# Windowed attention, cross attention and experts in one kernel: the order of row 0's and each pair's stack transfers

## The reference, cut to what matters

```python
x = x + pos_emb[:S][None]
w = x.reshape(B, nW, WIN, H, hd)                     # windows of 128 tokens, 16 heads of 16
attn = softmax(einsum('bnqhd,bnkhd->bnhqk', w, w) * scale)
local = einsum('bnhqk,bnkhd->bnqhd', attn, w)
comp = conv_general_dilated(x.transpose(0, 2, 1), conv_w, window_strides=(4,), ...) + conv_b
gt = concatenate([comp[:, :G], broadcast(global_memory)], axis=1)   # 64 compressed + 64 memory tokens
ga = softmax(einsum('bshd,bghd->bhsg', xm, gt) * scale)
glob = einsum('bhsg,bghd->bshd', ga, gt)
mix = sigmoid(concatenate([local, glob], -1) @ gate_w + gate_b)
return (mix * local + (1.0 - mix) * glob) @ out_w + out_b
```

## Time and profile before

| what | us |
|---|---|
| three timed runs | 1131.73, 1133.57, 1128.36 |
| median | 1131.73 |
| the profiled execution's own time | 1133.69 |
| its span, first to last instruction | 1131.9 |
| PE busy in the span | 1067.5 (94%) |
| self attention, to the first work of the cross attention's program | about 441 |

### The profile page before, as it was taken

One profiled execution on the slowest core, in us unless ns is written; L12 is line 12 of the kernel. 1 busy time (PEld: TensorE's weight loads), 2 busy tenths in 40 slices (PEclk: granted clock), 3 DMA queues, 4 the chain that ended last, 5 costly groups with the idle time before them and its releaser, 6 DMA issues.

```text
span 1131.9 us, 28588 instructions
## 1 busy us (share of the span) xinstructions
PE 1067.5 (94%) x11089; PEld 916.6 (81%) x11089; DVE 670.1 (59%) x1317; ACT 647.8 (57%) x872; POOL 554.5 (49%) x678
## 2 busy tenths in 40 slices
PE   7899999999999988999999997999999999999996
PEld 6777787777777766777777775898899999999995
DVE  4488888888888878788888886323324222222221
ACT  2366666665666665787777775444455444444441
POOL 5435355553445233433656665466754544444442
PEclk9899999999999999999999999999999999999999
DMA  8563634636355433665676557564432223332222
GB/s 215 150 180 98 184 107 125 166 94 169 110 137 139 123 96 72 173 170 165 150 165 176 145 159 250 142 138 51 43 54 48 48 48 48 52 52 48 48 43 24
DMA packets 174562, 130.22 MB, mean 115 GB/s; under 512 B 60810, under 2 KB 162927, under 8 KB 174432
## 3 DMA queue, kind: packets, MB, share of 16 engines
q1 hardware_dynamic: 155280, 106.79, 35.1%
q0 software_dynamic: 15840, 18.77, 11.6%
q10 hardware_dynamic: 3312, 2.85, 0.9%
HBM read 88.29 MB, written 40.08 MB: 113 GB/s over the span
## 4 chain that ended last, share of the span: by engine, by line
PE 51%; ACT 2%; issue 2%; another core or an unknown queue 2%; DMA 2%; POOL 1%; DVE 1%; POOLq 0%; ACTq 0%; SPq 0%
PE ps_scores L1990 22%; PE ps_out L2008 10%; PE ps_turn L1853 4%; PE ps_misc L1885 2%; PE ps_out L1865 2%; PE ps_misc L1806 2%; PE ps_scores L1840 2%; PE ps_misc L1873 1%; PE ps_turn L1969 1%; PE ps_scores L1833 1%; PE ps_scores L1914 1%; PE ps_misc L1879 1%; ACT weights L2181 1%; DMA weights<-q_scr 1%
## 5 line engine op out<-in xcount | busy, mean ns | idle before, releaser
L1990 PEld LDWEIGHTS ps_scores<-xgT,weights 128*128 128x128 f32 x2272 | 263.8, 192 | 9.2 <-ACT xgT L2205 3.4
L1990 PE MATMUL ps_scores<-xgT,weights 128*128 128x128 f32 x2272 | 266.1, 275 | 4.6 <-ACT xgT L2205 2.8
L2479 DVE TENSOR_TENSOR gate<-ps_scores,silu 128x512 f32<-128x512 f32 x71 | 49.1, 692 | 246.9 <-ACT silu L2221 222.7
L959 ACT ACTIVATE weights<-ps_scores 128x1024 f32<-128x1024 f32 x128 | 126.9, 1023 | 78.6 <-PE ps_scores L631 62.9
L2221 ACT ACTIVATE silu<-ps_scores 128x512 f32<-128x512 f32 x71 | 42.4, 597 | 210.6 <-PE ps_scores L1990 189.2
L2008 PE MATMUL ps_out<-w2s,gate 128*128 x560 | 132.6, 380 | 0.8 <-DVE y L2485 0.8
L2214 ACT COPY weights<-weights 128x2048 f32 x68 | 129.9, 1911 | 0.5 <-issue 0.3
L2008 PEld LDWEIGHTS ps_out<-w2s,gate 128*128 128x128 f32 x560 | 100.9, 190 | 12.0 <-issue 1.2
L1133 DVE TENSOR_REDUCE sa_rowmax<-ps_turn 128x8 bf16<-128x1024 f32 x64 | 77.8, 1215 | 36.7 <-PE ps_turn L608 36.7
L964 ACT CAST weights<-ps_scores 8x1024 bf16<-8x1024 f32 x64 | 64.3, 1005 | 56.0 <-PE ps_scores L622 56.0
L1676 POOL DMA_INDIRECT table<-entry,slot_i x64 | 65.0, 1016 | 38.8 <-issue 13.8
(11 more groups left out here) (325 smaller groups left out, 2115.4 us busy)
## 6 DMA issues: line engine op xcount, KB each, us to landing
weights<-w_scr SPq DMA_DIRECT2D x60, 256.0 KB, 3.9
weights<-q_scr SPq DMA_DIRECT2D x96, 128.0 KB
ks<-w_scr SPq DMA_DIRECT2D x24, 256.0 KB, 4.0
weights<-k_scr SPq DMA_DIRECT2D x48, 120.0 KB
w_scr<-wp SPq DMA_DIRECT2D x7, 768.0 KB, 3.8
q_scr<-qp SPq DMA_DIRECT2D x14, 384.0 KB
weights<-in_w1T SPq DMA_DIRECT2D x10, 512.0 KB
weights<-in_w3T SPq DMA_DIRECT2D x10, 512.0 KB
```

Source lines behind the costliest of these rows:

```text
L959: act.activation(probs[s % 2][:], m.scores[s % 2][:], ACT.Exp, scale=SCALE).then_inc(exped, 1)
L1990: mm = pe.matmul(h_ps[r % 2][:, j, c, :], weights[:, j, k, c * P:(c + 1) * P], xgT[r % 2][:, k, :], start=(k == 0), stop=(k == DT - 1))
```

## The change

1. Row 0's twelve w transfers become twenty-four of half the heads each (64 KB instead of 128 KB), half 0 first: nine from SP and three from ACT for half 0, ten and two for half 1. gs for row 0 likewise: twelve of 48 KB instead of six of 96 KB, half 0's six from ACT, half 1's three and three. `scores` and `queries_scores` of row 0 wait for their own half.
2. The first gp is split by DVE (`split_first_g`) instead of POOL, and stored by ACT instead of SP. `g_scr` lies as partition, half, token, so that its store has runs of 768 B instead of 384 B. PE turns the compressed tokens before the context; ACT copies them first.
3. SP's order in the prologue: row 1's parts are stored after all of row 0's transfers and the three gs transfers; the cross keys and values of row 0 before row 1's stacks; x of pair 2 and context 2 between row 1's query and key transfers.
4. In every later pair, `store_g` stands inside `stack_w`, between the six query and the six key transfers.
5. POOL scales gate_b and adds the first three output biases at the end of its work for row 0 instead of ahead of the loop.
6. The identity products are spread anew: 14, 8, 4, 7, 16, 34 and 3 become 6, 12, 4, 5, 14, 22 and 5.

```diff
+        def load_first_heads(queue, f, dst, scratch, parts, loaded, slots):
+            for s in slots:
+                queue.dma_start(dst[s:KS:SLOTS, f * HU:(f + 1) * HU, :],
+                                scratch[parts[s], f * P:(f + 1) * P, :].rearrange("(h d) t -> d h t", d=HD))\
+                    .then_inc(loaded(s), 16)
...
@@ stack_second_row
             stack(qs[0][:, :, 1, :], rows, Q_PARTS, w_stacked, 0, False)
+            load_x(2)
+            load_ctx(2)
             stack(ks[0][:, :, 1, :], rows, K_PARTS, w_stacked, 32, True)
@@ stack_w
             stack(qs[i].rearrange("k h r t -> k h (r t)"), w_scr[i], Q_PARTS, w_stacked, 64 * p, False)
+            store_g(p)
             stack(ks[i].rearrange("k h r t -> k h (r t)"), w_scr[i], K_PARTS, w_stacked, 64 * p + 32, True)
@@ sync_program
         store_first_pair(0, row0_stored)
-        stack_first_row()
+        sp.wait_ge(row0_stored, 16)
+        load_first_heads(sp, 0, first_qs, first_row, Q_PARTS, heads_of_row0(0), range(SLOTS))
+        load_first_heads(sp, 0, first_ks, first_row, K_PARTS, heads_of_row0(0), range(3, SLOTS))
+        load_first_heads(sp, 1, first_qs, first_row, Q_PARTS, heads_of_row0(1), range(SLOTS))
+        load_first_heads(sp, 1, first_ks, first_row, K_PARTS, heads_of_row0(1), range(4))
+        sp.wait_ge(g_stored, 16)
+        load_first_tokens(sp, 1, heads_of_g(1), range(3))
         store_first_pair(1, w_stored)
-        store_g(0)
-        load_first_g()
...
+        store_keys_values(0)
         stack_second_row()
-        store_keys_values(0)
-        load_ctx(2)
         for p in range(1, NP):
-            if p < NP - 1:
+            if 1 < p < NP - 1:
                 load_x(p + 1)
             stack_w(p)
-            store_g(p)
@@ gpsimd_program
-        split_g(0)
         split_k(0)
...
-        pool.wait_ge(rest_in, N_REST)
-        pool.tensor_scalar(gate_b[:], gate_b[:], 0.5, None, ALU.mult).then_inc(bias_set, 1)
-        for c in range(3):
-            add_out_bias(c)
         for b in range(NB):
...
+            if b == 0:
+                pool.wait_ge(rest_in, N_REST)
+                pool.tensor_scalar(gate_b[:], gate_b[:], 0.5, None, ALU.mult).then_inc(bias_set, 1)
+                for c in range(3):
+                    add_out_bias(c)
@@ scalar_program
-        load_first_slots(act, ks[0][:, :, 0, :], first_row, K_PARTS, row0_stacked, range(4))
-        copy_cT(0, whole_out)
+        load_first_heads(act, 0, first_ks, first_row, K_PARTS, heads_of_row0(0), range(3))
         copy_gT(0)
         first_g(0)
+        copy_cT(0, whole_out)
+        act.wait_ge(g_split, 3)
+        act.dma_start(g_scr[0].rearrange("c p k t -> p c k t"), gp[:]).then_inc(g_stored, 16)
...
-        load_first_slots(act, gs[0][:], g_scr[0], K_PARTS, g_stacked, range(3, SLOTS))
+        load_first_tokens(act, 0, heads_of_g(0), range(SLOTS))
+        load_first_heads(act, 1, first_ks, first_row, K_PARTS, heads_of_row0(1), range(4, SLOTS))
+        load_first_tokens(act, 1, heads_of_g(1), range(3, SLOTS))
```

More of the change, by code:

```diff
@@ L199, in self_attention @@
     w_scr = [nc.dram_tensor(f"w_scr{i}", [3, D, R * S], BF16, kind="Internal").ap() for i in range(2)]
-    g_scr = [nc.dram_tensor(f"g_scr{i}", [3, D, GK], BF16, kind="Internal").ap() for i in range(2)]
+    g_scr = [nc.dram_tensor(f"g_scr{i}", [3, P, DT, GK], BF16, kind="Internal").ap() for i in range(2)]
     x_first, first_in, conv_in, kv_in, rest_in = (
@@ L313, in load_g @@
                 sp.wait_ge(shifted, R * UPR * (p - 1))
-            stack(gs[i][:], g_scr[i], K_PARTS, g_stacked, 32 * p, False)
+            for s, part in enumerate(K_PARTS):
+                if s > 2:
+                    sp.wait_ge(g_stacked[s % 3], 32 * p + 16)
+                sp.dma_start(gs[i][s:KS:SLOTS].rearrange("d (k h) t -> d k h t", k=DT),
+                             g_scr[i][part].rearrange("(h d) k t -> d k h t", d=HD)).then_inc(g_stacked[s % 3], 16)
         def load_ctx(c):
@@ L583, in scores @@
             i = p % 2
-            if s == 0 and b == 0:
-                for loaded in row0_stacked:
-                    pe.wait_ge(loaded, 64)
+            if b == 0 and s in (0, 2):
+                pe.wait_ge(row0_stacked[f], FIRST_HEADS)
             elif s == 0:
@@ L601, in queries_scores @@
             i = p % 2
-            if s == 1:
+            if b == 0 and s == 1:
+                pe.wait_ge(row0_stacked[2], FIRST_GLOBAL)
+            elif s == (1 if b else 3):
                 for loaded in g_stacked:
@@ L750, in tensor_program @@
         pe.wait_ge(first_in, N_FIRST)
-        keep_warm(14)
+        keep_warm(6)
         turn_w(0, m.misc)
-        keep_warm(8)
+        keep_warm(12)
         turn_w(1, side[1])
@@ L761, in tensor_program @@
             compress(0, k)
+        turn_g(0)
         turn_c(0, whole_out)
-        turn_g(0)
-        keep_warm(7)
+        keep_warm(5)
         pe.wait_ge(kv_in, 2 * 16)
@@ L767, in tensor_program @@
         pe.wait_ge(dve_set, 1)
-        keep_warm(16)
+        keep_warm(14)
         scores(0, 0)
-        keep_warm(34)
+        keep_warm(22)
         for b in range(NB):
@@ L1211, in vector_program @@
         dve.tensor_scalar(m.neg_ident[:], m.ident[:], -1.0, None, ALU.mult).then_inc(dve_set, 1)
+        ones_of_g(0)
+        add_conv_bias(0)
+        split_first_g()
         dve.wait_ge(conv_in, N_CONV)
@@ L1215, in vector_program @@
             dve.tensor_copy(vg[i][g, :, 0:HD], memory[g, :].rearrange("p (h d) -> p h d", d=HD)).then_inc(dve_set, 1)
-        add_conv_bias(0)
-        for i in range(2):
-            dve.tensor_copy(gs[i][KS:, :, :].rearrange("j (f h) g -> j f h g", f=DT),
-                            m.ident[KS:KX_ROWS, KS:KX_ROWS].unsqueeze(1).unsqueeze(3).broadcast_to((HU, DT, HU, GK)))\
-                .then_inc(dve_set, 1)
         maxima(0, 0)
+        ones_of_g(1)
         apply_norm(2)
```

32 lines of the change are left out of this document (20 added, 12 removed).

## The result

The changed kernel takes 1165.58 us (median of 4 runs, 1161.45 to 1166.52). The kernel before took 1130.05 us beside it (4 runs, 1128.33 to 1133.57). The ratio is 1.0283, with a 95% interval of 1.0252 to 1.0315. The forecast was 1161 us, with a range of 1142 to 1178.

The account below looks back on a forecast made before the run. PE was taken as the bound, with a matmul under way for 94% of the span. -9.0 (start, biases) + 27.1 (store) + 10.5 (clock) = +28.6 on 1133.7 gives 1162.3; adjusted to the timed median, 1161 us, range 1142 to 1178.

Parts of the forecast that it names:

- Part 1, the start of row 0: Prologue: row 0's first global unit comes at 32.8 us instead of 36.90, a gain of 4.1 us, bounds 2 and 5.5.
- Part 2, the biases: Row 0: PE's 2.7 us wait and 2.2 us of lower clock go, a gain of 4.9 us, bounds 4 and 5.5.
- The sum: Whole kernel: -9.0 + 27.1 + 10.5 = +28.6 us on the profiled 1133.7, so 1162.3; stated as 1161.
- a new wait for row 1's w stack: Row 1: its w stack's last landing comes at 52 to 54 us; no cost, at worst 3 us.
- these -9.0 us: Prologue and row 0: start and biases together gain 9.0 us, bounds -11 and -3, carried into the whole sum.
- Part 3, the store between queries and keys: Pairs 1 to 7: SP's wait for the split delays keys and gs; PE waits 4.0 us a pair, 27.1 in all.
- The forecast chain of 17.8 us: Later pairs: store, six keys, small stores, context and six gs after POOL's split take 17.8 us, bounds 16 and 19.5.
- Part 4, the clock: Pairs 1 to 7: lower clock behind PE's waits in two pairs in three, 1.5 us a pair, 10.5 us in all.
- the 15.4 us that the prediction put on that case: Pairs 1 to 7: by the skill's rule the clock falls in all seven, 2.2 us each, 15.4 instead of 10.5.
- The rival in which the clock holds: Pairs 1 to 7: the wait comes but the clock stays up, +18 us, near 1150; chance 0.23.
- The rival on the other side: Later pairs: chain behind the split 14 us or less, nothing waits, prologue's gain stands, near 1124; chance 0.08.

Follow-up runs that it names:

- experiment 3: Kernel before with only POOL's gate_b scaling and first three output biases moved to the end of row 0's work: 1120.46 us, ratio 0.9972.
- experiment 2: Kernel before with only the gp store moved between query and key transfers: 1152.57 us, ratio 1.0244.
- experiment 1: Changed kernel with the gp store put back behind the key transfers: 1119.80 us against 1122.80 for the kernel before, ratio 0.9981.
- experiment 9: Changed kernel, gp store behind the keys, pair 1's w parts stored before row 1's keys have landed: 1116.15 us against 1117.96 before, ratio 0.9986.
- experiment 11: As experiment 9, with identity products ahead of row 1's first scores (nine) and pair 1's first global unit (eleven): 1124.57 us against 1128.35 before, ratio 0.9979.
- experiment 6: Changed kernel with the gp store behind the keys and x of pair 2 loaded behind row 1's keys: 1119.83 us, ratio 0.9981 to the kernel before.
- experiment 7: Changed kernel with POOL instead of SP issuing the later pairs' gp store, right behind the split: 1122.82 us, ratio 0.9995 to the kernel before.
- experiment 8: Changed kernel with POOL storing gp and x of pair 2 loaded behind row 1's keys: 1121.78 us, ratio 0.9989 to the kernel before.
- experiment 10: As experiment 9, with x of pair 2 also loaded behind row 1's keys: 1116.33 us, ratio 0.9992 to the kernel before.
- experiment 4: Changed kernel with identity products on PE in the waits of pairs 1 to 7 (five and nine): 1144.59 us, ratio 1.0188 to the kernel before.
- experiment 5: Changed kernel run again unedited: 1157.66 us against 1122.96 for the kernel before, ratio 1.0291.

## Why the prediction was right, and where it was off

**Part 1, the start of row 0 (forecast -4.1, bounds -2 and -5.5): right in kind, too small.** It gave 6.2 us, outside its bounds. The store of gp was issued at 21.57 where 22.4 was forecast, and landed in 2.9 us (24.46) where 4 were taken. The last of its six readers was issued at 27.69 and landed at 30.34, in 2.7 us. Their issue took 3.83 us, less than the 4.3 assumed. The Trainium skill (DMA: Bandwidth & Descriptors, Rules for kernel authors) says that many small transfers should be joined, as under 64 KB one pays mostly overhead. Read as a reason against this edit it is not borne out: the twelve gs transfers of 48 KB landed in 2.2 to 2.7 us, against 2.5 to 5.0 for the 96 KB ones of before, and the half heads of w in 2.2 to 3.3. But what was under way beside them was not the same, and no run halves the transfers alone, so how much of the 6.2 us comes from halving is not shown.

**Part 2, the biases (forecast -4.9): right in kind, a little less, and measured against one execution.** Alone they gave 4.1 us (experiment 3). The sum took row 0's wait of 2.71 us and its fallen clock as fixed; in experiment 2, with the same program there, the wait was 1.55 us and the clock held, and against that the biases gave 1.6. Both parts together stand at row 1's first scores as forecast, at 54.09 against 54.1. That is a sum of errors that cancel: 2.29 us of it is a new wait for row 1's w stack, which landed at 53.84, inside the forecast 52 to 54. It was priced at nothing, at worst 3.

**The step that failed: that these -9.0 us reach the end.** The sum carried them to the last row. Experiment 1, which has both and not the moved store, is 2.1 us faster than before by its ratio and not 9. The prediction looked for what is late next in row 1, and stopped there. These places in the time lines, in us, show where the lead goes (in brackets how much earlier than before):

| | before | experiment 1 | experiment 9 | experiment 11 |
|---|---|---|---|---|
| row 1's first scores | 63.15 | 54.33 (8.8) | 54.52 (8.6) | 55.14 (8.0) |
| pair 1's first global unit | 89.11 | 83.56 (5.6) | 83.01 (6.1) | 83.70 (5.4) |
| pair 2's | 137.41 | 133.18 (4.2) | 131.13 (6.3) | 131.74 (5.7) |
| pair 7's | 379.85 | 375.67 (4.2) | 373.45 (6.4) | 374.31 (5.5) |
| row 15's | 405.69 | 403.19 (2.5) | 400.96 (4.7) | 400.07 (5.6) |
| end of the self attention | 441.94 | 439.44 (2.5) | 437.21 (4.7) | 436.35 (5.6) |

In experiment 1 3.3 us go in pair 1's wait for gs, 1.3 behind it, where the clock is low, and 1.7 at row 15, where the clock fell before the output product and did not before. In experiment 9 the clock holds in pair 1, and in experiment 11 at row 15 too, and these two losses are not there; pair 1's remains. What pair 1 waits for is a chain of transfers, from its w store to its sixth gs transfer:

```profile
58.08 0.39 SPq L293 DMA_DIRECT2D w_scr<-wp  x1
...
81.64 5.32 SPq L265 DMA_DIRECT2D gs<-g_scr  x6
```

Before, its issue took 28.9 us, from 58.08 to 86.96. In experiments 1 and 6 to 11 it took 27.0 to 29.9 us, so the chain was about as long as before; but it began only 3.1 to 6.3 us earlier (51.80 to 55.00), where PE had come 8 to 10 us earlier. In the changed kernel it ends at 81.66 and in experiment 1 at 81.27, so pair 1's wait of 3.22 us there is hardly the moved store's doing: the pair's first global unit starts at 83.92, and at 83.56 in experiment 1.

**Part 3, the store between queries and keys (forecast 27.1): right in its mechanism.** It is shown three ways: the store moved alone makes the loss (2), the loss goes with it (1), and it goes too if only SP's wait goes (7). SP stood 6.6 us before it in a pair, where 6 were forecast. The forecast chain of 17.8 us was 18.8 in pair 3: the keys' issue 7.42 for 7.2, and the small stores and the context 3.7 for 2.3 (from 181.07 to 184.72), as the issue of the context took 2.30 us for 0.68. PE's waits were 3.5 us a pair for 4.0, in all 24.5 less the 1.2 of before, 23.3. They were shorter although the chain was longer, because the two costs overlap: in pair 3 the first global unit came 18.78 - 13.74 = 5.0 us later behind the split, of which 3.2 are PE's two waits (2.59 and 0.64). The rest went into work at the low clock between them, the output product's 3.28 us for 1.94 among it. Where the wait falls was given as the first global unit, with up to 1 us ahead of the first scores. In pairs 2, 3 and 4 nearly all of it fell ahead of the first scores (3.33, 2.59, 2.96), because the last key landed late: in pair 2 the sixth key transfer was issued at 126.94 and landed at 132.66, 5.7 us later.

**Part 4, the clock (forecast 10.5): right in size, by another count.** It was taken as two pairs in three at 2.2 us. It fell in all seven, behind waits of 2.59 to 3.49 us, at 1.4 us each in the first profile and 2.0 in the second (experiments 4 and 5); over the self attention filling was worth 10.4 and 15.4 us, and by the ratios 10.7 to 11.6. The Trainium skill (TensorE: Matmul & The Clock Gate, HAM oscillation) tells of a wait that recurs with every tile and brings the clock down every time, and so it was here in seven of seven; the 15.4 us that the prediction put on that case is the upper end of what was measured. The rival in which the clock holds is excluded.

**The sum, and how much of it is luck.** From row 1's first scores to the end of the self attention the forecast was 27.1 + 10.5 = 37.6, and it measured 36.7. With the -9.06 at its head that gives +27.6 at the end of the self attention, and +27.5 in the span, where +28.6 were forecast. But that 36.7 holds something that was not in the forecast: experiment 1, without the moved store, takes 385.11 us there, 6.3 more than before. So the moved store and its clock are worth 30.3 us in this profile (35.3 with the second one of the changed kernel), and the start 2.5 of its 9.0 us. By the ratios (1.0283 over 0.9981) the store costs 3.0%, about 34 us (29 to 39, an estimate from the two intervals), and the start gives 2.1. The start was taken some 6.5 us too good and the store 2 to 7 us too dear, and the two errors partly cancel. The ratio says more, 2.83% or 32 us, than the 27.8 between the two profiled executions; the one of before (1133.69) was slower than all four of its timed runs, and the one of after was the fastest of its four. So the forecast, which was summed on profiled executions, lies 4.6 us below the median. The rival on the other side needed a chain under 13.7 us and had 18.8.

**Left open.** Why pair 1's chain is not shortened, so that its first global unit starts at 82.5 to 84.4 us in experiments 1 and 6 to 11, is not settled. The chain was begun earlier (9), x was taken out of its way (6, 8), and neither brought it clearly forward. From 54 to 84 us the DMA engines are 69 to 75% busy in the changed kernel and in experiments 1 and 6 to 11, against 62% before, and in experiment 10 the early store landed slowly. That the transfers of the start compete is argued from these rows; no run took load away from the whole stretch. Nor does a run take the start apart: the halves, DVE's split, the layout of `g_scr` and the new spread of the identity products stand together in part 1. The moved store costs 2.44% on the old start and about 3.0% on the new one; the intervals overlap.

## What to carry to other kernels

A store that must wait for data, put ahead of transfers in a queue that is worked off in order, delays every one of them, and is worth its place only if the data are there when its turn comes; look up when they are ready before moving it, or have another engine issue it. A gain at the start is kept only if the next transfers that the bottleneck needs also come earlier: follow each stack to the first place where it was just in time, here one pair later, before a gain is carried to the end. Where a wait of about 3 us of TensorE recurred, the lower clock behind it cost another 1.4 to 2.0 us each time, and identity products in the waits gave that back. And look at a second profile of the old kernel before pricing a wait of it: one of 2.71 us was 1.55 in another execution with the same start.

## What the runs showed that was not expected

- **Waits and clock overlap.** Work at 1.2 GHz between two points of waiting shortens the second wait. So wait and clock can't be priced one by one: in pair 3 the slip was 5.0 us, with 3.2 of waits.
- **The same wait, two clocks.** Ahead of row 15's first scores PE waits 1.50 us for ACT before and after the change. Before (400.78 to 402.27) the clock stayed at 2.4 GHz, and the output product behind it took 1.94 us. In the changed kernel (at 428.20) the clock fell and it took 3.47. It fell there in experiments 1, 2, 5, 6, 7, 8 and 9 too, and not in 3 and 10, nor in 4 and 11, where earlier waits were filled. For waits for a transfer it is the same: it fell behind 2.59 us in pair 3 of the changed kernel, and held behind 2.61 in pair 1 of experiment 9. What decides it is open.
- **Small transfers.** Half heads (64 KB) landed in 2.2 to 3.3 us in the start, where the twelve full heads of before took 2.9 to 6.4. gp's store with its longer runs landed in 2.9 us, and that of before took 5.76, behind full heads and row 1's store; what the runs alone do is not shown.
- **A store from POOL costs POOL 0.84 us** (experiment 7), and nothing of PE's time here.
